# A block with causal attention: q's third parts and their stores go behind the first step's maxima, and a step's three rows of maxima go in one transfer

## The chip, the cores and the metric
The kernel runs on one core of one Trainium2 chip. The metric is the device time of one execution in microseconds; the time of a kernel is the median of its runs. Engines have queues of their own and run in the order written in the kernel; they meet through semaphores. TensorE multiplies matrices and transposes (PE in the profile, its weight loads PEld), VectorE is DVE, ScalarE is ACT, GpSimd is POOL, and SyncE (SP) issues nearly all DMA transfers.

## The reference
x is (2, 1024, 128): two batches of 1024 tokens, 16 heads of 8. In short:

```python
h = layernorm(x) * (1 + ca) + sa            # ca, sa, ga, cb, sb, gb: from silu(c) @ wmod
q, k, v = split(h @ qkv_w + qkv_b);  q, k = rotary(q), rotary(k)
attn = softmax(where(causal, q @ k.T / sqrt(8), -inf));  x = x + ga * ((attn @ v) @ out_w + out_b)
h = layernorm(x) * (1 + cb) + sb
x = x + gb * expert(h)                      # 8 experts of 64, one by argmax(h @ w_router); f = leaky(h @ w_fc) ** 2
```

## The kernel before
A **unit** is one batch b and one half of its 1024 query tokens; units are attended in the order (0,0), (0,1), (1,1), (1,0). A **step** is a unit and a group of 4 heads: 16 steps, of which 0 to 3 are unit (0,0), 4 to 7 unit (0,1). Scores are wanted close to float32, from bf16 matmuls. So q and k are each split into three bf16 parts that add up to the value, and the parts are stacked on partitions 0 to 71 of the tiles qst and kst, through a copy in HBM (qparts, kparts). Partitions 72 to 74 of qst hold the negated row maximum, again in three parts, against rows of ones in kst.

Each step has two passes. **Pass A** (`pass_a`, L1040 and L1045) makes the scores query by key, and VectorE reduces each PSUM bank of them to row maxima in tmax (L880). When the step's last bank is reduced, the stage `max1` makes negm (VectorE, L797) and splits it into three bf16 parts in negp, with four small operations of GpSimd (L535 to L538). The stage `max2` transposes negp (TensorE, L963), copies it to negt, 48 partitions by 128 (ScalarE, L631), and SyncE's `max_rows` sends negt to rows 72, 73 and 74 of qst (L450). **Pass B** (`pass_b`, L1062) makes the scores key by query with the maximum already taken off; ScalarE takes the exponential into pt (L676), GpSimd zeroes the future keys of diagonal blocks (L572), and `times_v` multiplies by v (L1082). TensorE's first matmul of pass B of a step waits for that step's rows of maxima.

`plan()` gives every bank of pass A (and of pass B) a **slot**, and every other stage a slot as well; each engine's queue is the slots in order, and within a slot the bank first, then the stages. Step 0 has the pass A slots 0 to 10, step 1 has 11 to 21, step 2 has 22 to 32. Pass B of step 0 takes slots 19 to 29, that of step 1 begins in slot 30. `max1` of step 0 is in slot 10, `max2` of step 0 in slot 16, `max1` of step 1 in slot 21, `max2` of step 1 in slot 25. TensorE does the matmuls of a stage one slot earlier, behind that slot's banks. Step 4 ends its pass A in slot 70; its pass B begins in slot 79, and v of unit (1,0) is in slot 82. Seven PSUM banks (`NB`) go round in the order in which TensorE uses them, whoever the user is: a bank can be written again when its user of seven places earlier has been read. Between slots without a bank of pass B TensorE does a filler matmul (L1024).

The stages q1, q2, q3 and k1, k2, k3 prepare a unit's q and k. q1: two matmuls (L952), two VectorE products into rot (L776), and their sum in full (GpSimd, L380). q2: cast to the first part (ScalarE, L619), remainder (GpSimd, L385). q3: cast to the second part (ScalarE, L623), remainder as the third part (GpSimd, L390), and the **stores** of q: `store` of SyncE waits for all three parts and issues eight transfers, two for each of the four groups of heads (L419 and L421). k is the same with four stores (L419). `load` brings a unit's stack from HBM to qst and kst, six transfers for a group (L441). For unit (0,1) the slots of these stages are written out by hand in `FIXED`; all others are looked for by `put`, which keeps GpSimd's longer stages apart. A stage of `FIXED` is placed where it says.

SyncE's queue is in the order of stages too: q3 of unit (0,1) (slot 8) with its eight stores, then the three rows of step 0 (slot 16), k3 (slot 22) with four stores, the three rows of step 1 (slot 25), the loads of group 0 (slot 25), and so on.

Of the kernel before, what the change touches and what calls it, by code (L numbers as in the profile page):

```python
# [29 lines left out]
P = 128  # L30
# [6 lines left out]
TU = HALF // P  # L37
HG = 4
NG = H // HG
PARTS = 3  # L40
ROWS = PARTS * PARTS * HD
ROWSM = ROWS + PARTS
# [30 lines left out]
def groups_b(half):  # L73

    out = []
    if half:
        out += [(kt, 0, 0, [(h, 1) for h in range(HG)]) for kt in range(TU)]
    for kt in range(TU):
        n = HALF - kt * P
        nh = max(1, HALF // n) if n < 384 else 1  # L80
        out.append((kt, half, kt * P, [(h, nh) for h in range(0, HG, nh)]))
    return out
# [17 lines left out]
POST_LAST = ["oT", "out", "st", "var2", "ln", "h2", "rt", "a0", "ohT", "a1", "m0", "a2", "m1", "a3", "m2", "y0", "m3", "y1"]  # L100
PREP_AT = [[0, 0], [40, 1], [93, 1]]
POST_AT = {("oT", (0, 0)): 81, ("a0", (0, 0)): 131}
FIXED = {("q1", (0, 1)): 3, ("q2", (0, 1)): 6, ("q3", (0, 1)): 8, ("k1", (0, 1)): 16, ("k2", (0, 1)): 19, ("k3", (0, 1)): 22}
MAX_LAG = 3
O_LAG = 3

# [12 lines left out]
def plan():  # L119
# [20 lines left out]
    def put(at, *stage):  # L140
# [3 lines left out]
        if need and stage[0] in HIDDEN + ("y0", "y1") and stage[1][0:2] == UNITS[-1]:  # L144
            hold = 1
        at = FIXED.get(stage, at)
        while stage not in FIXED and need and any(held.get(t, 0) + need > SIDES for t in range(at, at + hold)) \
                or stage not in FIXED and stage[0] != "max1" and any(t in pooled for t in range(at, at + busy)):
            at += 1
# [43 lines left out]
def adaln_block(nc, x, ct, wmod, wqkv, wsw, bcol, bv, wo, bo, wr, wfc, wpj, rope, out):  # L193
# [25 lines left out]
    with ExitStack() as ctx:  # L219
        def sb(name, shape, dt=F32):  # L220
            return ctx.enter_context(nc.sbuf_tensor(name, shape, dt))
# [4 lines left out]
        def sem(name):  # L226
            return ctx.enter_context(nc.semaphore(name))
# [45 lines left out]
        qst = sb("qst", [P, 2, H, HALF], BF16)  # L273
# [6 lines left out]
        negt = sb("negt", [PARTS * HG * TU, 2, P], BF16)  # L280
# [40 lines left out]
        s_mstack = [sem(f"s_mstack{i}") for i in range(2)]  # L321
# [19 lines left out]
        def side_ready(eng, st, k=0):  # L341
            ap, i, use = side(st, k)
            eng.wait_ge(s_side[i], use + 1)
            return ap, s_sfree[i]

        def wait_read(eng, name, u, k=0):

            _, i, use = side((name, u), k)
            eng.wait_ge(s_sfree[i], use + 1)

        def stored(eng, i, n, groups=0):

            eng.wait_ge(s_store[i], (2, 1)[i] * 16 * (NG * n + groups))
# [9 lines left out]
        def tiles(u):  # L363

            return PIECES[u[0:2]][u[2]]
# [27 lines left out]
        @block.sync  # L393
        def _(sp):
            sp.dma_start(xs[:, 0], x[0]).then_inc(s_ldx[0], 16)
            sp.dma_start(wqkv_sb[:, :], wqkv).then_inc(s_ldqkv, 16)
            sp.dma_start(wsw_sb[:, :], wsw).then_inc(s_ldqkv, 16)
            sp.dma_start(bcol_sb[:, :], bcol).then_inc(s_ldqkv, 16)
            for half in range(2):
                cols = slice(HALF * half, HALF * half + HALF)  # L400
                sp.dma_start(rope_sb[:, :, cols], rope[:, :, cols]).then_inc(s_ldrope[half], 16)
                if half == 0:
                    sp.dma_start(bv_sb[:, :], bv.partition_broadcast(P)).then_inc(s_ldbv, 16)
            for i in range(1, B * 2):
                sp.dma_start(xs[:, i], x[i]).then_inc(s_ldx[i], 16)
            sp.dma_start(bo_sb[:, :], bo.partition_broadcast(P)).then_inc(s_ldrest, 16)
            sp.dma_start(wo_sb[:, :], wo).then_inc(s_ldrest, 16)
            sp.dma_start(wr_sb[:, :], wr).then_inc(s_ldrest, 16)
            sp.dma_start(wfc_sb[:, :], wfc).then_inc(s_ldrest, 16)
            sp.dma_start(wpj_sb[:, :, :], wpj).then_inc(s_ldrest, 16)  # L410

            def store(u, i, groups):

                n, w = prep_no[u], 2 * u[0] + u[1]
                sp.wait_ge(s_part[i], 3 * (n + 1))
                for g in groups:
                    dst = (qparts, kparts)[i].ap()[w, g].rearrange("j d h t -> (d h) j t")
                    src = part[i][HG * HD * g:HG * HD * (g + 1)]
                    sp.dma_start(dst[:, 0:PARTS], src).then_inc(s_store[i], 16)  # L419
                    if i == 0:  # L420
                        sp.dma_start(dst[:, PARTS:5], src[:, 0:2]).then_inc(s_store[i], 16)  # L421

            def load(u, g):

                (b, half), w, n = u, 2 * u[0] + u[1], prep_no[u]
                if b:
                    sp.wait_ge(s_pv, group_no[(NG + g, len(groups_b(1)) - 1)] + 1)
                h0, row, R = HG * g, HG * HALF, PARTS * HD
                sp.wait_ge(s_ones, half + 1)
                sp.wait_ge(s_zeros, half + 1)  # L430
                if b:
                    sp.dma_start(qst[ROWS:ROWSM, half, h0:h0 + HG, :].rearrange("p h t -> p (h t)"),
                                 qst[ROWSM:ROWSM + PARTS, half, h0:h0 + HG, :].rearrange("p h t -> p (h t)")
                                 ).then_inc(s_stack[half][g], 16)
                for i, (dst, src, step) in enumerate(((qst, qparts, HD), (kst, kparts, 0))):
                    stored(sp, i, n, NG if n or g else 1)
                    planes = (5, PARTS)[i]
                    for p in range(PARTS):
                        rows = bass.AP(tensor=src, offset=((w * NG + g) * planes * HD + p * step) * row,
                                       ap=[[row, R], [1, HG * HALF]])  # L440
                        sp.dma_start(dst[R * p:R * p + R, half, h0:h0 + HG, :].rearrange("p h t -> p (h t)"),  # L441
                                     rows).then_inc(s_stack[half][g], 16)

            def max_rows(s):
                b, half, g = STEPS[s]
                wait_read(sp, "max2", s)
                M = HG * TU
                for p in range(PARTS):
                    dst = qst[ROWS + p:ROWS + p + 1, half, HG * g:HG * g + HG, :].rearrange("o h (r x) -> o (h r) x", x=P)
                    sp.dma_start(dst, negt[M * p:M * p + M, s % 2, :]).then_inc(s_mstack[s % 2], 16)  # L450

            def run(st):
                if st[0] in ("q3", "k3"):
                    first = st[1] == (0, 0)
                    store(st[1], 0 if st[0] == "q3" else 1, range(1 if first else NG))
                if st[0] == "load":
                    load(st[1], st[2])
                    if st[1:] == ((0, 0), 0):
                        for i in range(2):
                            store((0, 0), i, range(1, NG))  # L460
                if st[0] == "max2":
                    max_rows(st[1])
                if st[0] == "y1":
                    u, (t0, t1) = st[1], tiles(st[1])
                    wait_read(sp, "y1", u)
                    sp.dma_start(out[2 * u[0] + u[1], :, t0:t1], y[:, t0:t1]).then_inc(s_out, 16)

            for st in order:
                run(st)
            sp.wait_ge(s_out, 16 * sum(len(p) for p in PIECES.values()))  # L470
# [114 lines left out]
        def _(act):  # L585
# [22 lines left out]
            def run(st):  # L608
# [17 lines left out]
                if name == "max2":  # L626
                    s = u
                    src, free = side_ready(act, st)
                    if s >= 2:
                        act.wait_ge(s_mstack[s % 2], 48 * (s // 2))  # L630
                    act.activation(negt[:, s % 2, :], src[0:PARTS * HG * TU, 0:P // 2].bitcast(BF16),  # L631
                                   ACT.Copy).then_inc(free, 1)
                if name == "o":
                    s = u
# [43 lines left out]
            for st in PRE:  # L678
                run(st)
# [206 lines left out]
        def _(pe):  # L886
# [163 lines left out]
            def pass_b(i):  # L1050

                s, gi, (kt, kh, c0, _), (h0, nh), _ = b_at[i]
                b, half, g = STEPS[s]
                n, w = bank_no[i], HALF - c0
                if n == 0:
                    pe.wait_ge(s_ones, 1)
                if gi == 0 and h0 == 0:
                    pe.wait_ge(s_mstack[s % 2], 48 * (s // 2 + 1))
                dst = take("b", i)
                for j in range(nh):  # L1060
                    h = HG * g + h0 + j
                    last = pe.matmul(dst[:, j * w:(j + 1) * w], kst[:, kh, h, kt * P:kt * P + P],  # L1062
                                     qst[:, half, h, c0:HALF], start=True, stop=True)
                last.then_inc(s_b, 1)
# [89 lines left out]
```

## Time and profile before

| | us |
|---|---|
| median of 3 runs (lowest, highest) | 366.17 (365.56, 366.2) |
| the profiled execution | 365.83 |
| its span, first to last instruction | 364.1 |
| PE busy | 333.2 (92% of the span) |
| DVE busy | 257.9 (71%) |
| ACT busy | 207.7 (57%) |
| POOL busy | 110.9 (30%) |

The profiled execution is 1.7 us longer than its span. Busy time of PE is the time in which any matmul is open; matmuls overlap, so that their starts lie closer than their durations (a 512-column one has 0.38 us, and the next starts 0.22 us after it).

### The profile page before, as it was taken

The numbers are of one execution on the slowest core, as the hardware profiler recorded it, in microseconds if no ns is written. First come the engines' busy times: TensorE is split into PE (matmuls) and PEld (weight loads), VectorE is DVE, ScalarE is ACT, GpSimd is POOL, SyncE is SP. The second block draws the span as 40 slices with busy tenths as digits, with TensorE's granted clock in tenths as the row PEclk, the third lists the DMA queues.
The fourth block names the chain that finished last, engine by engine and source line by source line (L and its number), as shares of the span: only waits on it lengthen the run. The fifth ranks groups of instructions, "written<-read, shape, count | busy, mean of one in ns | idle before, by whom it ended". The sixth has DMA issues, their size and how long they took to land.

```text
span 364.1 us, 6867 instructions
## 1 busy us (share of the span) xinstructions
PE 333.2 (92%) x2320; PEld 163.3 (45%) x2360; DVE 257.9 (71%) x563; ACT 207.7 (57%) x399; POOL 110.9 (30%) x191
## 2 busy tenths in 40 slices
PE   6999779998889899999999989999999999899886
PEld 3645335443443333453543535444435445435555
DVE  3764787888899987777777888677888777423254
ACT  5160146755157565778456765864777666686241
POOL 3927453437401413601301212101204132344121
PEclk9999989999999999999999999999999999999999
DMA  6527704220510003140220400400000000000000
GB/s 208 181 62 198 169 23 111 69 66 2 139 46 0 3 1 74 42 137 0 69 81 17 119 16 2 136 0 31 1 2 3 3 3 1 4 0 3 29 2 29
DMA packets 13362, 18.97 MB, mean 52 GB/s; under 512 B 4216, under 2 KB 9208, under 8 KB 13328
## 3 DMA queue, kind: packets, MB, share of 16 engines
q1 hardware_dynamic: 13040, 18.14, 18.6%
q8 instruction: 19, 0.31, 0.4%
q10 hardware_dynamic: 288, 0.39, 0.3%
q14 instruction: 15, 0.12, 0.1%
HBM read 12.98 MB, written 5.24 MB: 50 GB/s over the span
## 4 chain that ended last, share of the span: by engine, by line
PE 60%; issue 9%; DVE 9%; POOL 3%; ACT 3%; another core or an unknown queue 2%; SPq 1%; DMA 1%; ACTq 0%; POOLq 0%; DVEq 0%
PE ps_o L1082 16%; PE ps L1045 13%; PE ps L1062 12%; PE ps L1016 4%; DVE tmax L880 4%; PE ps L1003 4%; PE ps L1040 2%; PE ps L952 1%; ACT pt L676 1%; PE ps L1009 1%; PE ps L1024 1%; DVE rot L776 1%; PE ps L943 1%; DMA qst<-negt 1%
## 5 line engine op out<-in xcount | busy, mean ns | idle before, releaser
L880 DVE TENSOR_REDUCE tmax<-ps 128x1 f32<-128x512 f32 (+3 forms) x304 | 185.7, 655 | 60.1 <-PE ps L1045 57.7
L676 ACT ACTIVATE pt<-ps 128x512 f32<-128x512 f32 (+1 forms) x304 | 161.3, 576 | 100.0 <-PE ps L1062 86.3
L1045 PE MATMUL ps<-kst,qst 128*128 128x128 bf16 (+3 forms) x566 | 110.1, 273 | 4.3 <-DVE tmax L880 2.4
L1062 PE MATMUL ps<-qst,kst 128*128 128x512 bf16 (+3 forms) x368 | 105.2, 326 | 5.8 <-DVE rot L776 1.8
L1082 PE MATMUL ps_o<-pt,v_sb 128*32 128x512 f32 (+3 forms) x768 | 78.7, 496 | 2.7 <-ACT pt L676 1.4
L1045 PEld LDWEIGHTS ps<-kst,qst 128*128 128x128 bf16 x576 | 49.6, 99 | 65.7 <-DVE tmax L880 16.1
L572 POOL TENSOR_SCALAR_AFFINE_SELECT pt<-pt 128x512 f32<-128x512 f32 x64 | 40.2, 638 | 65.1 <-ACT pt L676 64.7
L1062 PEld LDWEIGHTS ps<-qst,kst 128*128 128x128 bf16 x384 | 35.0, 98 | 32.1 <-issue 8.0
L1024 PE MATMUL ps<-maska,identb 128*128 128x512 bf16 x120 | 35.4, 402 | 3.5 <-POOL maska L491 3.3
L535 POOL CAST negp<-negm 128x16 bf16<-128x16 f32 x16 | 3.1, 196 | 92.5 <-DVE negm L797 92.3
L1082 PEld LDWEIGHTS ps_o<-pt,v_sb 128*32 128x32 f32 x768 | 16.9, 108 | 29.2 <-ACT pt L676 16.3
L1040 PE MATMUL ps<-maska,identb 128*128 128x512 bf16 x54 | 21.2, 392 | 0.4 <-DMA kst<-kparts 0.4
L516 POOL TENSOR_TENSOR rstd<-veps,mhalf 128x4 f32<-128x4 f32 (+1 forms) x9 | 8.5, 949 | 37.1 <-DVE veps L738 36.9
L1024 PEld LDWEIGHTS ps<-maska,identb 128*128 128x128 bf16 x124 | 12.6, 103 | 15.6 <-POOL maska L491 3.3
L1003 PE MATMUL ps<-h2t,wfc_sb 128*128 128x512 f32 (+1 forms) x40 | 16.9, 520 | 0.0
L856 DVE TENSOR_TENSOR fg<-ps,fg 128x512 f32<-128x512 f32 (+1 forms) x20 | 11.4, 578 | 7.6 <-PE ps L1009 4.6
L619 ACT ACTIVATE part<-full 128x512 bf16<-128x512 f32 x8 | 5.0, 628 | 20.6 <-POOL full L380 15.4
L1016 PE MATMUL ps<-wpg,fg 128*128 128x128 f32 x128 | 16.1, 279 | 0.6 <-DVE fg L856 0.6
L1016 PEld LDWEIGHTS ps<-wpg,fg 128*128 128x128 f32 x128 | 15.1, 192 | 3.1 <-ACT pt L676 1.7
L380 POOL TENSOR_TENSOR full<-rot 128x512 f32<-128x512 f32 x6 | 7.6, 1266 | 25.2 <-DVE rot L776 25.2
L655 ACT ACTIVATE fg<-ps 128x512 f32<-128x512 f32 (+1 forms) x20 | 10.3, 513 | 2.2 <-PE ps L1003 1.9
L776 DVE SCALAR_TENSOR_TENSOR rot<-ps,bcol_sb,rope_sb 128x512 f32<-128x512 f32 x16 | 11.3, 742 | 0.0
(103 smaller groups left out, 259.3 us busy)
## 6 DMA issues: line engine op xcount, KB each, us to landing
qst<-qparts SPq DMA_DIRECT2D x48, 96.0 KB
kst<-kparts SPq DMA_DIRECT2D x48, 96.0 KB
qparts<-part SPq DMA_DIRECT2D x16, 96.0 KB, 1.9
kparts<-part SPq DMA_DIRECT2D x16, 96.0 KB, 1.9
xs<-in_x SPq DMA_DIRECT2D x4, 256.0 KB, 7.2
rope_sb<-in_rope SPq DMA_DIRECT2D x2, 512.0 KB, 6.3
qparts<-part SPq DMA_DIRECT2D x16, 64.0 KB, 1.8
qst<-negt SPq DMA_DIRECT2D x48, 4.0 KB, 1.7
```

Source lines behind the costliest of these rows:

```text
L572: pool.affine_select(out=d, in_=d, compare_op=ALU.is_ge, fill=0.0, base=0, pattern=[[0, HG], [1, P]], channel_multiplier=-1).then_inc(s_tr ...
L676: act.activation(pt[:, G % NP, h0:h0 + nh, 0:w], src, ACT.Exp, scale=SCALE).then_inc(s_exp, 1)
L776: dve.scalar_tensor_tensor(out=rot[i][:, j], in0=src, scalar=bcol_sb[:, 2 * i + j:2 * i + j + 1], in1=rope_sb[:, j, HALF * u[1]:HALF * u[1 ...
L856: dve.tensor_tensor(fg[:, c, cols], src[:, cols], fg[:, c, cols], ALU.mult).then_inc(free, 1)
L880: dve.tensor_reduce(dst, src, AX.X, ALU.max).then_inc(s_max, 1)
L1003: pe.matmul(dst[:, cols], wfc_sb[:, P * c:P * c + P], h2t[:, cols], start=True, stop=True).then_inc(full_, 1)
L1016: last = pe.matmul(dst[:, D * t:D * t + D], fg[:, c, P * t:P * t + P], wpg[:, u[0], c], start=(c < c1), stop=(c == c1))
L1024: pe.matmul(ps[:, reached[0] % NB, :], identb[:, :], maska[:, :, :].rearrange("p h k -> p (h k)"), start=True, stop=True)
L1040: pe.matmul(dst, identb[:, :], maska[:, :, :].rearrange("p h k -> p (h k)"), start=True, stop=False, skip_group_check=True)
L1045: last = pe.matmul(dst[:, j * nk:(j + 1) * nk], qst[:, half, h, r * P:r * P + P], kst[:, kh, h, k0:k0 + nk], start=(kind != "diag"), stop= ...
L1062: last = pe.matmul(dst[:, j * w:(j + 1) * w], kst[:, kh, h, kt * P:kt * P + P], qst[:, half, h, c0:HALF], start=True, stop=True)
L1082: last = pe.matmul(ps_o[32 * j:32 * j + 32, 0, c0:HALF], v_sb[:, TU * (2 * b + kh) + kt, c:c + 32], pt[:, G % NP, j, 0:HALF - c0], start=( ...
```

## The change
There are two edits. In `FIXED`, q3 of unit (0,1) goes from slot 8 to slot 18. This moves ScalarE's cast to the second part, GpSimd's remainder and SyncE's eight stores behind `max1` and `max2` of step 0; on GpSimd the remainder is now between k1's sum and k2's remainder, on SyncE the stores are just ahead of k3's. Nothing else changes its slot. In `max_rows`, the loop over three transfers of one row (16 partitions of negt each) becomes one transfer of three rows (48 partitions), for all 16 steps; the semaphore rises by 16 instead of 48 and its two waiters follow.

```diff
-FIXED = {("q1", (0, 1)): 3, ("q2", (0, 1)): 6, ("q3", (0, 1)): 8, ("k1", (0, 1)): 16, ("k2", (0, 1)): 19, ("k3", (0, 1)): 22}
+FIXED = {("q1", (0, 1)): 3, ("q2", (0, 1)): 6, ("q3", (0, 1)): 18, ("k1", (0, 1)): 16, ("k2", (0, 1)): 19, ("k3", (0, 1)): 22}
...
             def max_rows(s):
                 b, half, g = STEPS[s]
                 wait_read(sp, "max2", s)
-                M = HG * TU
-                for p in range(PARTS):
-                    dst = qst[ROWS + p:ROWS + p + 1, half, HG * g:HG * g + HG, :].rearrange("o h (r x) -> o (h r) x", x=P)
-                    sp.dma_start(dst, negt[M * p:M * p + M, s % 2, :]).then_inc(s_mstack[s % 2], 16)
+                dst = qst[ROWS:ROWSM, half, HG * g:HG * g + HG, :].rearrange("p h (r x) -> p (h r) x", x=P)
+                sp.dma_start(dst, negt[:, s % 2, :]).then_inc(s_mstack[s % 2], 16)
...
-                        act.wait_ge(s_mstack[s % 2], 48 * (s // 2))
+                        act.wait_ge(s_mstack[s % 2], 16 * (s // 2))
...
-                    pe.wait_ge(s_mstack[s % 2], 48 * (s // 2 + 1))
+                    pe.wait_ge(s_mstack[s % 2], 16 * (s // 2 + 1))
```

## Rows read from the trace of the kernel before

**Rows 1.** The page, busy time, share of the span, instructions
```profile
PE 333.2 (92%) x2320; PEld 163.3 (45%) x2360; DVE 257.9 (71%) x563; ACT 207.7 (57%) x399; POOL 110.9 (30%) x191
```
**Rows 2.** Waits of PE, whole span: us in total, times, longest
```profile
PE ps L1062 <- DMA qst<-negt: 1.3, 1, 1.3
```
**Rows 3.** Timeline, PE, 40 to 60 us: start, us, [idle before <-releaser]
```profile
43.05 0.24 PE L963 MATMUL ps<-identb,negp 128*48 128x128 bf16 x1 [2.42 <-POOL negp L538]
...
46.51 0.33 PE L1045 MATMUL ps<-kst,qst 128*128 128x384 bf16 x1
49.08 0.37 PE L1045 MATMUL ps<-kst,qst 128*128 128x384 bf16 x1 [2.25 <-DVE tmax L880]
...
53.24 0.24 PE L963 MATMUL ps<-identb,negp 128*48 128x128 bf16 x1
...
58.75 0.34 PE L1045 MATMUL ps<-kst,qst 128*128 128x384 bf16 x1
59.22 0.39 PE L1062 MATMUL ps<-qst,kst 128*128 128x512 bf16 x1
```
**Rows 4.** Windows of 0.5 us: us, PE busy, PEclk, DMA share, GB/s
```profile
47.50:48.00 0.50, 0.00 (x0) 1.00 0.06 8
...
49.00:49.50 0.50, 0.42 (x2) 0.72 0.00 0
...
52.50:53.00 0.50, 0.50 (x9) 0.86 0.00 0
```
**Rows 5.** Timeline, DVE, 40 to 50 us
```profile
40.27 0.19 DVE L797 TENSOR_REDUCE negm<-tmax 128x16 f32<-128x32 f32 x1
...
45.46 0.69 DVE L880 TENSOR_REDUCE tmax<-ps 128x2 f32<-128x512 f32 x1 [2.01 <-PE ps L1045]
46.07 1.40 DVE L776 SCALAR_TENSOR_TENSOR rot<-ps,bcol_sb,rope_sb 128x512 f32<-128x512 f32 x2
47.38 1.61 DVE L880 TENSOR_REDUCE tmax<-ps 128x4 f32<-128x512 f32 x3
```
**Rows 6.** Timeline, POOL, 40 to 52 us
```profile
40.85 1.15 POOL L390 TENSOR_TENSOR part<-rot,part 128x512 bf16<-128x512 f32 x1 [0.80 <-ACT part L623]
41.95 0.20 POOL L535 CAST negp<-negm 128x16 bf16<-128x16 f32 x1
...
42.78 0.22 POOL L538 TENSOR_TENSOR negp<-negr,negp 128x16 bf16<-128x16 f32 x1
47.60 1.26 POOL L380 TENSOR_TENSOR full<-rot 128x512 f32<-128x512 f32 x1 [4.60 <-DVE rot L776]
50.54 1.16 POOL L385 TENSOR_TENSOR rot<-full,part 128x512 f32<-128x512 f32 x1 [1.68 <-ACT part L619]
```
**Rows 7.** Timeline, ACT, 43 to 51 us
```profile
43.33 0.27 ACT L631 ACTIVATE negt<-ps 48x128 bf16<-48x128 bf16 x1 [2.62 <-PE ps L963]
49.28 0.60 ACT L676 ACTIVATE pt<-ps 128x512 f32<-128x512 f32 x1 [5.68 <-remote]
49.77 0.62 ACT L619 ACTIVATE part<-full 128x512 bf16<-128x512 f32 x1
50.29 1.07 ACT L676 ACTIVATE pt<-ps 128x512 f32<-128x512 f32 x2
```
**Rows 8.** Timeline, SP, DMA issues, 42 to 56 us (eight L419 and L421, first shown)
```profile
42.03 0.32 SPq L419 DMA_DIRECT2D qparts<-part  x1
...
45.78 1.88 SPq L450 DMA_DIRECT2D qst<-negt  x3
54.44 1.75 SPq L419 DMA_DIRECT2D kparts<-part  x4
```
**Rows 9.** The chain that ended last, at 57 us: start, us, what
```profile
57.43 1.74 DMA qst<-negt
```
**Rows 10.** Timeline, PE, 101 to 103 us
```profile
101.14 0.39 PE L1062 MATMUL ps<-qst,kst 128*128 128x512 bf16 x1 [1.32 <-DMA qst<-negt]
...
102.68 1.16 PE L956 MATMUL ps<-wqkv_sb,ht 128*128 128x128 f32 x8
```
**Rows 11.** Timeline, DVE, from 98 us
```profile
98.36 5.46 DVE L880 TENSOR_REDUCE tmax<-ps 128x1 f32<-128x512 f32 x9
```

## The prediction
> **What bounds the kernel now.** I read the page first, for how much TensorE time there is: matmuls are open for 92% of the span [rows 1]. A place where TensorE stands still is therefore paid for in full unless another engine is as late there. Then I read the waits of TensorE for the change's own transfer: the trace names one, of 1.3 us [rows 2]. A list of releasers can hide what stands at the head of a queue, so I read TensorE in order of time around the first step [rows 3]. The reader is to see two pauses. The transposition of step 0's maxima (L963) comes 2.42 us late, released by GpSimd. Then nothing starts between the last matmul of pass A at 46.51 and 49.08; the trace names VectorE, but VectorE had handed on that bank long before. What lies ahead of it in TensorE's queue is slot 19's first matmul of pass B, which waits for the rows of maxima. The third of those transfers starts about 1.2 us after 45.78 and lands 1.74 us after that [rows 8, 9], at some 48.8; the 49.08 agrees. The granted clock falls right behind this pause, in the half microsecond from 49.0 (0.72), and is back only after 52.5 [rows 4].
>
> So step 0's maxima are one chain: VectorE's last reduction, four small GpSimd operations, transpose, copy by ScalarE, rows to qst. Three links of it are late. On GpSimd the q remainder (L390, 40.85 to 42.00) stands ahead of them though the maxima are there at 40.46 [rows 5, 6]. On SyncE eight stores of q stand ahead of the rows: the copy is ready at 43.60 [rows 7], the first row is issued at 45.78 [rows 8]. And there are three issues, 1.88 us, instead of one.
>
> **The move, up to the rows of step 0.** With q3 in slot 18, GpSimd is free at 40.46. Its handover from VectorE is 0.13 us elsewhere (46.07 + 1.40 = 47.47 to 47.60) [rows 5, 6], so the split of the maxima starts at 40.59 instead of 41.95: 1.36 us earlier. TensorE's transpose comes at 41.69, ScalarE's copy ends at 42.24, and SyncE has nothing else to issue: the row transfer starts at 42.27. With k1's matmuls shifted alike, TensorE comes to slot 19's pass B at 46.51 + 0.16 - 1.36 = 45.3.
>
> **The transfer.** 1.74 us is the landing of a 4 KB row [rows 9]. What one of 12 KB with 48 packets takes the trace does not show. Below: the same 1.74, if it spreads over 16 engines as each row does. Above: while three rows move, the 16 engines are busy 0.06 of the time at 8 GB/s [rows 4]; that is 0.48 engine-us for 16 packets of 256 B, 0.03 us each. With 16 packets in a row on one engine 0.45 us come on top (2.2 us), with all 48 on one 1.4 us (3.2 us). Today the third row lands 2.9 us after the first issue. I take 1.74 to 2.2: landed at 44.0 to 44.5, ahead of 45.3 in either case. The Trainium skill, DMA: Bandwidth & Descriptors, section on why a DMA increments its semaphore by 16, states that the number of engines is the largest up to 16 that divides the slowest dimension of both sides; here those are 3 and 48, so three engines where each old row had 16. It speaks against merging; by it the landing is the 2.2 us, and the sum below loses 0.04 us.
>
> **What is late next.** The pause was also time in which others caught up, so I follow all queues to step 1's transpose. VectorE reduces bank 16 at 45.46 - 1.36 = 44.10, does k1's two products until 46.11, then banks 17 to 19 (1.61 us) and 20, 21 (0.5 us each), and has step 1's maxima at 48.8 [rows 5]. GpSimd: k1's sum (L380, 1.26 us) from 46.24 to 47.50; now the moved q remainder (L390, 1.15) to 48.6; k's first remainder (L385, 1.16) to 49.75; then step 1's four small operations (41.95 to 43.00, 1.05 us) to 50.8 [rows 6]. ScalarE: exponentials of slot 19 near 45.8; then its cast of k (L619, 0.62) must wait for GpSimd's 47.50, which it did not before, and the exponentials of slots 20 and on stand behind it until 48.15, which is still 2.1 us earlier than before [rows 7]. Its moved cast of q (L623, 0.6 us like L619) stands in the gap behind the copy, before slot 19, and costs nothing; that gap is from 42.24 to 45.7. TensorE runs out of banks on the way several times by 0.1 to 0.5 us and then waits for step 1's split: its second transpose comes at 50.85 instead of 53.24 [rows 3]. The shift is **2.39 us**, set by GpSimd's queue, no longer by TensorE. If the q remainder were not in this queue it would be more by up to 1.15.
>
> SyncE: q's eight stores take 3.75 us (42.03 to 45.78) [rows 8]. Now they run from 48.65 to 52.40, with nothing behind them but k's stores. Those waited for GpSimd's k3 before; GpSimd ends L385 at 49.75 instead of 51.70, so they start at 54.44 - 1.95 = 52.5 and end at 54.3. The one row transfer of step 1 starts there and lands at 56.1 to 56.5. Before, it landed at 57.43 + 1.74 = 59.17 and TensorE, through with its pass A of 58.75 (0.16 us in the stream), could have gone on at 58.91 but did at 59.22 [rows 3, 9]. With the shift it asks at 56.52. So this wait of **0.31 us** goes too, or all but 0.04 of it. The loads of unit (0,1) stand behind this on SyncE; they come earlier too.
>
> **Later steps.** At 101.14 stands the one wait that the trace puts on the rows, 1.32 us [rows 2, 10]. One transfer lands 0.7 to 1.2 us earlier. I count this at **zero**: VectorE has nine reductions without a gap from 98.36 to 103.82, the banks that TensorE takes next come free only through them, and v's matmuls at 102.68 take the bank of slot 79, whose reduction is the seventh of these (about 102.0 to 102.6) [rows 10, 11]. If that cover is not as tight as I read it, up to 0.5 us more is won. The other thirteen row transfers show no wait; a shorter one is worth nothing there. After step 1 the order of work is the old one on all queues and nothing is tied to absolute time, so the shift should last to the end.
>
> **Sum.** 2.39 + 0.31 + 0 = 2.7 us. The profiled execution is 365.83 us with a span of 364.1; I expect a span of 361.4. Against the median of the runs, 366.17, that gives 363.5.
>
> **The rivals.** (a) *The clock.* The one pause before 43.05 left the clock at full, the second one brought it down [rows 3, 4]. Afterwards there are pauses of 1.1 us (before 41.7) and, from 45.5 to 50.85, several small ones with a last one of about 1.7 us; only half of that stretch is matmul work. If the clock falls there and stays low as long as it did (49.2 to 52.6, 3.4 us), up to 3.4 us of matmuls run at half speed where TensorE is the bound again: 1.7 us back, 365.2. Against it: a pause of 2.4 us alone did not do it. The Trainium skill, TensorE: Matmul & The Clock Gate, Part 1, says the same way round that activity releases a throttle which is the default. (b) *A queue longer than I make it.* From 46 to 51 GpSimd is busy nearly all the time, and ScalarE waits for it; if handovers or a bank cost 1 us more, the gain is 1.4 to 1.9 us: 364.5. (c) *Hidden anyway.* If the merged transfer or a later stretch bound by VectorE takes the gain, the time is 366.0. For it speaks only that step 4 does so locally; against it, that VectorE itself starts earlier. (d) *Slower: the merged transfer is slow.* It decides at 2.9 us from issue to landing, what three rows take now. At 3.2 us (all packets on one engine) no step loses more than 0.3 us. At 4.5 us each of the 16 steps would be up to 1.6 us later; if four of them have no slack, 6.4 are paid against 2.7 won: 369.9; two such steps give 366.7. No row has a transfer this small at such a time.
>
> **Chances.** Forecast (363.5, own range 362.6 to 364.3) 0.62; (a) 0.15; (b) 0.12; (c) 0.06; (d) 0.05. Some 0.2%, 0.7 us, is what a measurement can tell here; (a) and (b) are below 365.44 and count as faster: 0.89 faster, 0.06 same, 0.05 slower. The range goes down by the 0.5 us of step 4 and a shorter GpSimd queue, up to (a): 362.6 to 365.2.
>
> **What would show it.** Step 0's negp cast right behind the negm reduction, about 40.6; one row issue at 42.3; the first exponential at about 45.8 instead of 49.28; clock at 1.00 through 49 to 53; L390 of q between L380 and L385 at 47.5; second transpose near 50.9, no wait at the pass B of step 1. Landing of qst from negt between 1.7 and 2.2. VectorE still without a gap from 96 to 101. The forecast is wrong if the clock falls behind 46, if landing is above 2.9, or if the distance between the traces at 60 us is not there any more at the end.

## The result, and the profile after

| | before | after |
|---|---|---|
| median of five runs (lowest, highest) | 366.17 (365.29, 366.92) | 363.12 (361.05, 363.51) |
| the profiled execution | 365.83 | 361.05 |
| its span | 364.1 | 359.3 |
| PE busy | 333.2 | 334.0 |

The ratio is 0.9924, with an interval of 0.9895 to 0.9952: 1.8 to 3.8 us faster. 363.5 was forecast. But the two profiled executions differ by 4.8 us of span, not by 2.7, so the first question is where the rest lies. The timeline of PE at the start of the kernel, before (first fence) and after (second); columns as in [rows 3]:

```profile
6.30 1.71 PE L924 MATMUL ps<-silu,wmod_sb 128*128 128x2 f32 x8
7.86 1.87 PE L1024 MATMUL ps<-maska,identb 128*128 128x512 bf16 x4
```
```profile
6.29 0.95 PE L922 MATMUL ps<-silu,wmod_sb 128*128 128x2 f32 x8
7.10 1.02 PE L1022 MATMUL ps<-maska,identb 128*128 128x512 bf16 x4
```

Line numbers of after are lower by two. The same eight matmuls start at the same time and take 1.71 us in one execution and 0.95 in the other. This is long before anything that the change touches, and it carries on: VectorE reduces step 0's maxima at 40.27 before and at 37.56 after, 2.71 us apart. The kernels below, most of which have the move or the merged transfer too, speak against an effect of the change (last section). So from here on all times are counted from this reduction of step 0, called **zero** below; what the change does is read from the distances behind it.

The timelines of DVE, SP, ACT, POOL and PE after, the lines that answer to [rows 5], [rows 8], [rows 7], [rows 6] and [rows 3]:

```profile
37.56 0.19 DVE L795 TENSOR_REDUCE negm<-tmax 128x16 f32<-128x32 f32 x1
...
45.82 0.19 DVE L795 TENSOR_REDUCE negm<-tmax 128x16 f32<-128x32 f32 x1
```
```profile
39.49 0.88 SPq L448 DMA_DIRECT2D qst<-negt  x1
45.87 0.34 SPq L419 DMA_DIRECT2D qparts<-part  x1
...
49.80 1.89 SPq L419 DMA_DIRECT2D kparts<-part  x4
51.74 0.77 SPq L448 DMA_DIRECT2D qst<-negt  x1
```
```profile
42.95 0.60 ACT L674 ACTIVATE pt<-ps 128x512 f32<-128x512 f32 x1 [2.97 <-PE ps L1060]
44.76 0.63 ACT L617 ACTIVATE part<-full 128x512 bf16<-128x512 f32 x1 [1.21 <-POOL full L380]
45.29 1.55 ACT L674 ACTIVATE pt<-ps 128x512 f32<-128x512 f32 x3
```
```profile
43.47 1.26 POOL L380 TENSOR_TENSOR full<-rot 128x512 f32<-128x512 f32 x1 [4.60 <-DVE rot L774]
44.68 1.16 POOL L390 TENSOR_TENSOR part<-rot,part 128x512 bf16<-128x512 f32 x1
45.80 1.16 POOL L385 TENSOR_TENSOR rot<-full,part 128x512 f32<-128x512 f32 x1
46.90 0.20 POOL L533 CAST negp<-negm 128x16 bf16<-128x16 f32 x1
```
```profile
38.92 0.24 PE L961 MATMUL ps<-identb,negp 128*48 128x128 bf16 x1 [1.00 <-POOL negp L536]
...
48.00 0.24 PE L961 MATMUL ps<-identb,negp 128*48 128x128 bf16 x1 [1.51 <-POOL negp L536]
...
53.52 0.34 PE L1043 MATMUL ps<-kst,qst 128*128 128x384 bf16 x1
54.02 0.39 PE L1060 MATMUL ps<-qst,kst 128*128 128x512 bf16 x1 [0.17 <-DMA qst<-negt]
```

The first transposition stands 1.36 us behind zero; before it was 2.78. The rows leave at 1.93. From 46.90 on step 1's own four operations follow GpSimd's three long ones without a gap, and the second transposition stands at 10.44, where it was 12.97: 2.53 us. The windows of 1 us around it (columns: stretch, us, busy time of PE, PEld, DVE, ACT and POOL, then PEclk, DMA share and GB/s as in [rows 4]) have the clock at full throughout, also behind the pause of TensorE:

```profile
46.00:47.00 1.00, 0.49 (x5) 0.21 (x5) 1.00 (x3) 0.86 (x3) 1.00 (x2) 1.00 0.25 59
47.00:48.00 1.00, 0.00 (x0) 0.00 (x0) 0.80 (x2) 1.00 (x3) 0.78 (x5) 1.00 0.54 134
48.00:49.00 1.00, 1.00 (x11) 0.60 (x15) 0.18 (x1) 0.39 (x2) 1.00 (x2) 1.00 0.69 171
```

The chain that ended last has the merged transfer of step 1, and PE at step 4 the wait that answers to [rows 10]; the third fence is DVE there [rows 11]:

```profile
51.26 0.44 SPq L419
51.69 0.04 issue
51.74 2.24 DMA qst<-negt
53.98 0.05 issue
54.02 0.39 PE ps L1060
```
```profile
95.26 0.39 PE L1060 MATMUL ps<-qst,kst 128*128 128x512 bf16 x1 [0.64 <-DMA qst<-negt]
...
97.49 1.16 PE L954 MATMUL ps<-wqkv_sb,ht 128*128 128x128 f32 x8 [0.20 <-DVE tmax L878]
```
```profile
92.57 6.06 DVE L878 TENSOR_REDUCE tmax<-ps 128x1 f32<-128x512 f32 x10
```

At step 1's first matmul of pass B the traces are 2.49 us apart (18.95 and 16.46 behind zero), at step 4's reduction of maxima 2.48, at step 15's 2.45. Nothing is given back in between. From the last reduction to the end this execution loses 0.36 us (323.83 against 321.74 from zero to the end, 2.09 apart; the second profile of the same kernel below has 2.28). 2.71 of the start and 2.09 behind zero are the 4.8 us.

The 0.36 us are lost behind the kernel's last instruction that the view shows, SyncE's last store of the result. The timelines of SP at the end, before and after:

```profile
361.12 1.22 SPq L466 DMA_DIRECT2D out<-y  x2
```
```profile
355.95 1.23 SPq L464 DMA_DIRECT2D out<-y  x2
```

From the end of this row to the end of the span there are 1.76 us before (362.34 to 364.1) and 2.12 after (357.18 to 359.3). All seven profiles of kernels with the merged transfer, the six below and this one, have 2.08 to 2.17 us there; all four with three transfers have 1.73 to 1.78. So the merged transfer costs some 0.35 us at the end of the program. Why it does is not shown.

### The profile page after: what moved, and what is told of

Read it like the earlier page. It is cut to its first block, busy times and chain, and to the rows that moved or that the text cites. A ratio compares the mean times of both kernels' runs of the same rounds, so it can differ in the third digit from the quotient of the medians.

```text
span 359.3 us, 6875 instructions
## 1 busy us (share of the span) xinstructions
PE 334.0 (93%) x2360; PEld 160.3 (45%) x2360; DVE 258.5 (72%) x563; ACT 207.7 (58%) x399; POOL 111.0 (31%) x191
## 4 chain that ended last, share of the span: by engine, by line
PE 64%; DVE 10%; issue 10%; POOL 2%; ACT 2%; SPq 1%; DMA 1%; ACTq 0%; DVEq 0%; POOLq 0%
PE ps_o L1080 17%; PE ps L1060 13%; PE ps L1043 13%; PE ps L1014 4%; DVE tmax L878 4%; PE ps L1001 4%; PE ps L1038 3%; PE ps L950 2%; PE ps L1022 1%; PE ps L1007 1%; DVE rot L774 1%; PE ps L941 1%; SPq L419 1%; ACT pt L674 1%; PE ps L968 1%
## 5 line engine op out<-in xcount | busy, mean ns | idle before, releaser
L1060 PE MATMUL ps<-qst,kst 128*128 128x512 bf16 (+3 forms) x384 | 110.3, 326 | 4.7 <-DVE rot L774 2.2
L1043 PE MATMUL ps<-kst,qst 128*128 128x128 bf16 (+3 forms) x576 | 113.2, 274 | 0.7 <-DVE fg L854 0.3
L570 POOL TENSOR_SCALAR_AFFINE_SELECT pt<-pt 128x512 f32<-128x512 f32 x64 | 40.3, 639 | 64.5 <-ACT pt L674 64.2
L1022 PE MATMUL ps<-maska,identb 128*128 128x512 bf16 x124 | 35.4, 393 | 3.3 <-POOL maska L489 3.3
L1038 PE MATMUL ps<-maska,identb 128*128 128x512 bf16 x64 | 24.5, 382 | 0.2 <-DVE tmax L878 0.2
```

What stands on the lines that cost most here:

```text
L570: pool.affine_select(out=d, in_=d, compare_op=ALU.is_ge, fill=0.0, base=0, pattern=[[0, HG], [1, P]], channel_multiplier=-1).then_inc(s_tr ...
L1022: pe.matmul(ps[:, reached[0] % NB, :], identb[:, :], maska[:, :, :].rearrange("p h k -> p (h k)"), start=True, stop=True)
L1038: pe.matmul(dst, identb[:, :], maska[:, :, :].rearrange("p h k -> p (h k)"), start=True, stop=False, skip_group_check=True)
L1043: last = pe.matmul(dst[:, j * nk:(j + 1) * nk], qst[:, half, h, r * P:r * P + P], kst[:, kh, h, k0:k0 + nk], start=(kind != "diag"), stop= ...
```

## The experiments

In the table each kernel's profiled execution, counted from zero: the two transpositions of step 0's and step 1's maxima (T0, T1), step 1's first matmul of pass B (B1), and how much earlier than in the kernel before step 4's and step 15's reductions of maxima come. Then the time, against runs of the kernel before of the same series. Those had a median of 365.89 beside change_again, move_only, merge_only and q_slot16, 365.96 beside k_late, k_late_rows3 and warm_wait, and 364.69 beside q_slot16_b and k_later, so medians of different series are not to be compared directly.

| kernel | zero at | T0 | T1 | B1 | step 4 | step 15 | median | ratio |
|---|---|---|---|---|---|---|---|---|
| before | 40.27 | 2.78 | 12.97 | 18.95 | 0 | 0 | 366.17 | |
| the change | 37.56 | 1.36 | 10.44 | 16.46 | 2.48 | 2.45 | 363.12 | 0.9924 (0.9895 to 0.9952) |
| change_again | 38.05 | 1.36 | 10.46 | 16.30 | 2.63 | 2.64 | 361.72 | 0.9904 (0.9869 to 0.9939) |
| move_only | 40.17 | 1.36 | 10.46 | 17.11 | 1.82 | 1.82 | 362.27 | 0.9915 (0.9883 to 0.9948) |
| merge_only | 39.76 | 2.78 | 11.80 | 17.60 | 1.33 | 1.34 | 365.18 | 0.9981 (0.9958 to 1.0003) |
| q_slot16 | 39.84 | 1.36 | 10.18 | 15.94 | 3.00 | 2.97 | 361.9 | 0.9893 (0.9858 to 0.9928) |
| q_slot16_b | 39.87 | 1.36 | 10.19 | 15.97 | 2.96 | 2.89 | 362.67 | 0.9925 (0.99 to 0.995) |
| k_late | 39.86 | 1.36 | 9.63 | 15.93 | 2.74 | 2.71 | 361.47 | 0.9895 (0.9864 to 0.9927) |
| k_late_rows3 | 37.82 | 1.37 | 9.63 | 15.94 | 2.71 | 2.66 | 362.88 | 0.9905 (0.9872 to 0.9938) |
| k_later | 39.88 | 1.37 | 9.64 | 14.43 | 3.61 | 3.56 | 362.21 | 0.9921 (0.9893 to 0.9949) |
| warm_wait | 39.68 | 2.79 | 12.43 | 18.89 | -0.06 | -0.84 | 366.65 | 1.0031 (1.0 to 1.0062) |

The medians are blunter than the distances, because the start of the kernel scatters by some 2 us (last section). Where they can't tell two kernels apart, the distances decide below, and that is said. In k_late, k_late_rows3 and k_later the first matmul of pass B of step 1 has no record; its start is taken as 0.22 us ahead of the matmul of pass A behind it (k_late 56.01, k_late_rows3 53.98, k_later 54.53). In k_late and k_late_rows3 v's matmuls stand ahead of B1 and in k_later behind it, so that B1 is not to be compared with the others'.

**The whole change again**, unchanged, to see what repeats.

> The changed kernel again, beside the three others on one chip. Both theories: 10.4 us from step 0's negm to the second transpose and 16.5 to pass B of step 1, whatever the start of the kernel does. The time of the profiled execution had 2.7 us of its 4.8 us from before step 0's maxima, where the change does nothing; the theory is that this is TensorE's clock coming up at another moment (11 us before, 6.3 us after by the matmul durations), and that the five times fall in two groups 2 us apart as they did (361.05, 361.57 and 363.12, 363.32, 363.51). Rival: the change itself makes the start faster; then the profile shows negm of step 0 at 37.6 again in every run of it, and those of the kernel before at 40.3.

Measured: 1.36, 10.46, 16.30 at B1 and 2.63 at step 4. The list of waits has none of TensorE for step 1's rows here, but there still is one of 0.17 us. PE:

```profile
54.02 0.34 PE L1043 MATMUL ps<-kst,qst 128*128 128x384 bf16 x1
54.35 0.39 PE L1060 MATMUL ps<-qst,kst 128*128 128x512 bf16 x1
```

TensorE could have gone on at 54.02 + 0.16 = 54.18. The rows were issued at 52.06; with the 2.24 us of the first profile they land at 54.30, and 0.05 us later the matmul starts, as at 54.02 in that profile. The rows left 14.01 us behind zero here and 14.18 there, where one store of q took 0.60 us of SyncE instead of 0.43 and the four of k 1.89 instead of 1.81. So the distances of one kernel repeat within 0.2 us (2.45 and 2.64 at step 15). The zero of 38.05 is early again, as the rival has it; the last section comes back to that. The times are 361.36 to 361.85 in four executions and 363.41 and 363.45 in two.

**The move alone:**

```diff
-... ("q3", (0, 1)): 8, ...
+... ("q3", (0, 1)): 18, ...
```

> The move alone: q3 of unit (0,1) in slot 18, three transfers of one row per step as before. I count from step 0's negm reduction, so that what lies before it drops out: to the second transpose it was 12.97 us before and 10.44 with both edits; to the first matmul of pass B of step 1 18.95 and 16.46. Theory (the GpSimd queue sets the second transpose, the three rows of step 0 are in time anyway: last one landed at 45.2 in the clock of the old profile, wanted at 45.3): 10.4 to 10.6 to the transpose, the same as with both. Pass B of step 1 then waits for the third row behind k's stores, about 0.7 us later than with both: 17.2. Time 0.6 to 0.8 us above the change, about 364.0 beside 366.2. Rival (merging and moving are worth about the same, each its part): the transpose comes only about 1.2 us sooner than before, 11.7, time near 364.9.

Measured: 1.82 us at step 4 and constant, clock 1.00; T1 is where the whole change has it, as the theory says. The chain that ended last at step 1:

```profile
54.30 0.51 SPq L450
...
54.85 0.59 SPq L450
...
55.50 1.74 DMA qst<-negt
57.24 0.05 issue
57.28 0.39 PE ps L1062
```

TensorE waits 0.81 us for the third row. Its zero is at 40.17, like that of the kernel before: the moved stage alone does not bring the early start.

**The merged transfer alone:**

```diff
-... ("q3", (0, 1)): 18, ...        # of the kernel after
+... ("q3", (0, 1)): 8, ...
```

> The merge alone: q3 stays in slot 8, its eight stores ahead of step 0's rows. Theory: the row transfer is issued as late as before and lands 2.24 us after issue (measured with the change) against 2.9 for the third of three, so pass B of step 0 starts 0.7 us sooner; to the second transpose 12.2 to 12.4 us instead of 12.97, to pass B of step 1 about 18.0 instead of 18.95; nothing at step 4. Time 0.7 to 1.0 us below the kernel before, about 365.3. Rival (the shorter pause keeps TensorE's clock at full, and that is the larger part): to pass B of step 1 under 17.3, time 1.6 us or more below. Rival (the merged transfer is on three engines and slower than it saves): no gain, 366.2.

Measured: T1 1.17 us sooner than before, where the theory had 0.6 to 0.8, and 1.33 at step 4. The pause of TensorE still lasts from 46.00 to 47.68, but the clock does not fall behind it, as the windows of 2 us show:

```profile
46.00:48.00 2.00, 0.64 (x4) 0.22 (x3) 2.00 (x5) 0.00 (x0) 0.91 (x1) 1.00 0.05 12
48.00:50.00 2.00, 2.00 (x19) 1.22 (x17) 1.97 (x6) 1.91 (x4) 1.00 (x2) 1.00 0.04 8
...
349.00:353.00 4.00, 4.00 (x14) 2.50 (x13) 0.98 (x7) 2.30 (x7) 0.32 (x1) 0.57 0.00 0
```

To split the 1.17: slot 19's first matmul of pass B has no record in the trace of before. The matmul behind it starts at 49.08 [rows 3], and in merge_only those two starts are 0.22 us apart (47.68 and 47.90), so it stood at some 48.86, 8.59 behind zero. Here it stands at 7.92: 0.67 us from the transfer. The other 0.50 come by T1, in the stretch that ran at the lower clock before: 0.63 us for a 512-column matmul there, 0.38 here. The last line shows that this execution met the lower clock elsewhere, in its tail. From step 15's reduction to the end it loses 1.55 us against before, 1.17 of them at the lower clock and the rest behind the last store, so that its end is 0.21 us later than that of before (324.04 against 323.83 from zero). The median's ratio, 0.9981, leaves open whether merging alone is faster at all; by the distances it is, up to the tail.

**q's third parts in slot 16** instead of 18, everything else as after, run twice:

```diff
-... ("q3", (0, 1)): 18, ...
+... ("q3", (0, 1)): 16, ...
```

> The change with q3 of unit (0,1) in slot 16 instead of 18: still behind step 0's maxima and rows on every queue, but ahead of k1's sum on GpSimd, where the queue stood empty for 4.6 us. Theory (the GpSimd queue between k1's sum and step 1's maxima sets the second transpose): L390 of q leaves that queue, 1.15 us; the transpose comes at 9.3 to 9.4 us from step 0's negm (10.44 with the change), where VectorE's negm of step 1 (8.26) is the bound; to pass B of step 1 15.2 to 15.4 (16.46). Time 1.1 us below the change, about 362.0. Rival (TensorE's banks through ScalarE's exponentials behind its cast of k set it): no difference from the change beyond 0.2 us.

> q3 in slot 16 again, beside the other on one chip, because its gain over the change (0.3 to 0.5 us by negm of step 4) is below what the times of one series tell. Theory (GpSimd's queue, 0.3 us of it q's remainder): second transpose at 10.18 again and step 4's negm 2.97 us ahead of the kernel before. Rival (the 0.3 us was a chance of one profile): 10.4 and 2.5 to 2.6.

Measured: T1 at 10.18 and 10.19, 3.00 and 2.96 us at step 4. The timeline of POOL:

```profile
42.41 1.16 POOL L390 TENSOR_TENSOR part<-rot,part 128x512 bf16<-128x512 f32 x1 [1.26 <-ACT part L621]
45.75 1.26 POOL L380 TENSOR_TENSOR full<-rot 128x512 f32<-128x512 f32 x1 [2.18 <-DVE rot L774]
47.81 1.16 POOL L385 TENSOR_TENSOR rot<-full,part 128x512 f32<-128x512 f32 x1 [0.80 <-ACT part L617]
48.91 0.20 POOL L533 CAST negp<-negm 128x16 bf16<-128x16 f32 x1
```

The remainder now lies in GpSimd's idle time ahead of k1's sum. That takes 1.16 us out of the queue behind it, yet T1 gains only 0.26: between k's sum and k's remainder GpSimd waits 0.80 us for ScalarE's cast of that sum. In the changed kernel q's remainder filled just that wait. The theory (T1 at 9.3 to 9.4) had it cost its whole duration in slot 18; that falls. B1 is 0.33 to 0.52 us sooner than after's two profiles, because the stores are out of the way too. The medians of the two runs of this kernel, 361.9 and 362.67, lie between the two of the change, 361.72 and 363.12, so they can't tell the kernels apart.

**k behind step 1's maxima too** (merged transfer; k_late_rows3 is the same slots with the three transfers of before):

```diff
-... ("q3", (0, 1)): 18, ("k1", (0, 1)): 16, ("k2", (0, 1)): 19, ("k3", (0, 1)): 22}
+... ("q3", (0, 1)): 16, ("k1", (0, 1)): 16, ("k2", (0, 1)): 22, ("k3", (0, 1)): 25}
```

> Built on the change: q3 of unit (0,1) in slot 16, k2 from 19 to 22 and k3 from 22 to 25, so that GpSimd has nothing of k between k1's sum and the split of step 1's maxima, and step 1's row transfer is ahead of k's four stores on SyncE. With q3 in slot 16 alone the second transpose came 10.18 us after step 0's negm, not at the 9.35 that I expected: GpSimd waited 0.80 us for ScalarE's cast of k, which the q remainder had filled before. Theory: k2's remainder and that wait are what is left, VectorE's negm of step 1 (8.26) becomes the bound; second transpose at 9.3 to 9.4, pass B of step 1 at 15.1 to 15.3, time 0.7 us below q3 in slot 16 alone. Rival: k's late preparation holds something else up (v of unit (0,1) moves from slot 27 to 30, the loads of unit (0,1) from 25 to 26), and the gain is gone by the first load or by step 4: no difference in time from q3 in slot 16.

> The same slots as the run before it, with three transfers of one row per step as in the kernel before. It asks what merging is worth once no stores stand ahead of the rows of steps 0 and 1. Theory: nothing; the third row lands some 2.9 us after the first issue instead of 2.24, and at step 0 and step 1 both are in time (pass B of step 0 at 5.0 us, of step 1 at 15.1 to 15.3 from step 0's negm), so the two differ by less than 0.3 us in time. Rival: the 0.66 us later landing holds up pass B of step 1 or a later step: 0.4 to 0.7 us slower than with one transfer.

Measured: T1 at 9.63 in both, 1.36 us behind step 1's reduction of maxima (8.27), just as T0 is behind step 0's. So VectorE, not GpSimd's long operations, sets it now; the 9.3 to 9.4 expected left too little for the split. But only 2.74 and 2.71 us are left at step 4, less than with q3 in slot 16 alone: the rival came true. PE of k_late has a new wait:

```profile
53.01 0.39 PE L1060 MATMUL ps<-qst,kst 128*128 128x128 bf16 x4
53.85 0.85 PE L1080 MATMUL ps_o<-pt,v_sb 128*32 128x384 f32 x8 [0.46 <-POOL pt L570]
```

k's last remainder (GpSimd, 51.97 to 53.13) now stands ahead of a diagonal block's mask, and the multiplication by v waits for that mask. And once step 1's rows have no stores ahead of them, merging gains nothing that can be measured at step 4 (0.03 us). From zero to the end k_late is even the longer one, 321.54 us against 321.18, by the 0.35 us or so behind the last store.

**k's last remainder two slots later still**, behind that mask:

```diff
-... ("k3", (0, 1)): 25}             # of k_late
+... ("k3", (0, 1)): 27}
```

> The k_late kernel with k3 of unit (0,1) in slot 27 instead of 25 (v of that unit goes to slot 32 with it). With k3 in slot 25 the second transpose came 9.63 us after step 0's negm, bound by VectorE's negm of step 1 as expected, but from step 3's negm on it stood at 2.71 us ahead of the kernel before, less than the 2.97 with q3 in slot 16 alone; its profile has a wait of 0.46 us of TensorE's multiplication by v for GpSimd's mask, which stood behind k3's remainder. Theory: k3 two slots later lets that mask through first; second transpose unchanged at 9.6, step 4's negm 3.2 to 3.5 us ahead of the kernel before. Rival: the wait only moves to another mask or to v, and step 4's negm stays at 2.7 to 2.8.

Measured: T1 the same, the wait for the mask is gone, 3.61 us at step 4 (3.2 to 3.5 expected) and 3.56 at step 15, 320.62 from zero to the end. By the distances this is the best of the kernels, about 1 us ahead of the change. The times don't settle it: its median of 362.21 is 0.46 us below that of q_slot16_b in its series, less than either kernel scatters. In its PE timeline the multiplication by v has no wait any more:

```profile
53.36 0.85 PE L1080 MATMUL ps_o<-pt,v_sb 128*32 128x384 f32 x8
54.14 0.71 PE L1043 MATMUL ps<-kst,qst 128*128 128x384 bf16 x2
```

**The old pause kept warm.** Before, with nine filler matmuls (no part of the result) put into the pause, to measure what the clock alone was worth:

```diff
+                if i == min(b_at):
+                    keep_warm(9)
                 if i in b_at:
                     pass_b(i)
```

> The kernel before with nine filler matmuls of 512 columns on TensorE between pass A of slot 19 and the first matmul of pass B, about 1.9 us inside the 2.2 us in which it waits for the rows. No wait is shortened. It measures what the fall of the clock behind that pause is worth. Theory (the clock is a small part of the gain; the second transpose was held by GpSimd behind the late exponentials): clock at full from 49 to 53 us; pass B of step 0 unchanged at 8.97 us from negm; second transpose at 12.3 to 12.7 instead of 12.97; time 0.3 to 0.7 us below the kernel before. Rival (much of what the change won is the clock kept at full): second transpose under 12.0, time 1 us or more below.

Measured: clock 1.00 from 46 to 54 us, slot 19's first matmul of pass B at 8.54 (the expectation's 8.97 is the second one; here it stands at 8.92), T1 at 12.43 instead of 12.97. With 8.59 for before that is 0.49 us for the clock, the same as merge_only gave. It is not all that TensorE wins: its last matmul ahead of T1 starts at 10.99 instead of 12.71, and then it waits 1.11 us for GpSimd's split, which comes at the old time. At B1 0.06 us is left. The timelines of PE there and at step 4, and SP at step 4:

```profile
58.57 0.39 PE L1062 MATMUL ps<-qst,kst 128*128 128x512 bf16 x1 [0.61 <-DMA qst<-negt]
...
101.37 0.39 PE L1062 MATMUL ps<-qst,kst 128*128 128x512 bf16 x1 [2.08 <-DMA qst<-negt]
```
```profile
97.67 2.53 SPq L450 DMA_DIRECT2D qst<-negt  x3
```

The stores of k and three row issues do not come sooner with TensorE, so the gain is lost in the wait for step 1's rows. At step 4 the three issues happened to take 2.53 us here, where they take 1.77 in the trace of before; the wait grew by the same 0.76, from 1.32 [rows 10] to 2.08, and from step 5 on the kernel is 0.66 us later than up to step 4. The cover that holds step 4's wait of 1.3 us at no cost does not hold 2.1. The time was expected 0.3 to 0.7 us below the kernel before and was not: 366.65 against 365.96, ratio 1.0031. The profile explains the end of its own execution only. In nine of the twelve executions the mean clock was below 1 (0.991 or 0.995), so in most of them it fell somewhere all the same; no trace shows where, and why the median is higher stays open.

## Why the prediction was right, and which terms were not

**How close the number is.** The time was forecast at 363.5 and measured at 363.12. A part of that is luck. The five executions of the change were two of 361.05 and 361.57 and three of 363.12 to 363.51; the median is one of the upper three, and the same kernel gave 361.72 the next time. The distances are the better test: of 2.70 us forecast, 2.45 and 2.64 are there at step 15 and 2.09 and 2.28 at the end.

**The bound and the pause.** Right: the pause behind pass A was the transfer of step 0's rows behind q's stores. merge_only shortens it by the transfer alone and move_only by the queue alone, and both move T1.

**The move.** Rows were forecast to leave 2.00 us behind zero and left at 1.93; GpSimd's order and the handover of ScalarE's exponentials came as worked out (the exponentials go on at 7.73 behind zero, forecast 7.9). The shift of the second transposition was 2.39 us by forecast and 2.53 in the trace, set by GpSimd's queue as said: TensorE stands idle for 1.51 us ahead of it and is released by L536, the last of GpSimd's four operations. Some 0.5 us of this shift is the clock that no longer falls, by warm_wait and merge_only; the kernel before had that loss in its T1. The side remark that the queue would gain "up to 1.15 more" without q's remainder is wrong in size: 0.26, since 0.80 us of waiting for ScalarE's cast takes its place (q_slot16). I had counted k's first remainder as ready to start when the remainder of q ended, and that hid the wait. Nor do the prediction's own times allow 1.15: with step 1's maxima at 48.8, a handover of 0.13 and a split of 1.05 the transposition comes at 50.0 at the earliest, 0.8 us sooner than 50.85.

**The transfer: the number is right, the reason is not.** The merged one landed after 2.24 us, near the upper value of 1.74 to 2.2, where one row takes 1.74 [rows 9] and still does in move_only. The upper value was 0.45 us for 16 packets in a row on one engine. Windows of 0.1 us (stretch, us, PEclk, DMA share, GB/s) show how long the data moves, first for step 0's merged transfer after, then for the third row of step 4 before:

```profile
41.00:41.10 0.10, 1.00 0.23 51
41.10:41.20 0.10, 1.00 0.24 54
```
```profile
100.60:100.70 0.10, 1.00 0.16 26
100.70:100.80 0.10, 1.00 0.12 16
```

By the trace's records of single packets, the 48 packets of the merged transfer run in three streams, 0.014 us from one packet of a stream to the next, with three packets of 4 bytes at their ends; a row's 16 packets have 16 of 4 bytes. That fits three engines where a row has 16. By the Trainium skill, DMA: Bandwidth & Descriptors, section on why a DMA increments its semaphore by 16, the dimensions 3 and 48 give three engines; the trace agrees with it. But the split costs little. At step 1 the merged transfer has its first packet 1.40 us after issue, moves data for 0.27 and lands 0.57 after that; a row has 1.23, 0.16 and 0.35. So of the 0.50 us only 0.11 is data on fewer engines; 0.17 lies ahead of the first packet and 0.22 behind the last. That 0.45 was so near is luck. What the other 0.39 us come from is open, as no transfer of the same bytes over 16 engines was run. Its issue takes 0.70 to 0.77 us (0.88 at step 0), against 0.51 to 0.59 for each of three rows that take 1.77 together.

**Step 1's wait: the term that was mis-sized.** The prediction has "this wait of 0.31 us goes too, or all but 0.04 of it". It measures -0.04 us in the first profile (2.53 at T1, 2.49 at B1) and +0.14 in the second. TensorE came to it as forecast: pass A at 53.52 + 0.16 = 53.68, 5.68 us behind T1, forecast 5.67. But the rows left 14.18 behind zero where 14.0 was forecast, landed 2.24 later instead of 1.74 to 2.2, and T1 was 0.14 us earlier than forecast, so that TensorE asked at 16.12 for what landed at 16.42. In the second profile the rows left at 14.01, as forecast, and the wait is 0.17 us. The forecast had it at nothing or 0.04. Two chains meet here. One runs through GpSimd and TensorE's queue, the other through k's stores on SyncE, and both moved by about 2.5 us; the later one still is SyncE's, as it was before. So the gain up to step 4 is 2.48 to 2.63, where 2.70 was forecast; 0.07 to 0.22 too much.

**The end: a term that was missing.** The prediction says that the shift should last to the end. It lasts to the last store; behind it each kernel with the merged transfer is some 0.35 us longer than those with three. So 2.09 and 2.28 us remain of 2.70.

**Step 4 at zero.** Right: TensorE's wait fell from 1.32 to 0.64 us and the distance did not change; VectorE goes through ten reductions without a gap (92.57 to 98.63, for the nine of [rows 11]), and v waits for its bank. The prediction looked only for what could be won there. warm_wait suggests, from one profile, that something could be lost: three issues that take 0.76 us longer cost 0.66. One transfer gives that place some margin.

**The rivals.** (a) The clock did not fall behind the new pauses, 1.00 in all profiles of the change. What it had cost before at T1 is measured twice, 0.50 and 0.49 us. It was no term of its own in my sum, and needed none, since GpSimd's queue sets T1 once it is gone. (b) and (c) fall by the distance of 2.5 to 2.6 us that is constant up to step 15. (d) falls by the 2.24 us; it would have decided at 2.9. That the change speeds up the start of the kernel, which both its profiles would suggest, is weakened by k_late_rows3, which has the early start too, and by the change's own executions, of which five of eleven took the longer times; it is not ruled out by a profile of the change with a late start.

**Are the two parts worth their sum?** No: 1.82 and 1.33 alone, 2.5 to 2.6 together. Both shorten the same wait at step 0. Added to the move, the transfer is worth 0.66 to 0.81 up to step 4 (step 1's third row), of which 0.29 and 0.48 are left at the end (322.03 us from zero with the move alone, 321.74 and 321.55 with both). With step 1's stores out of the way as well it wins 0.03 and loses 0.36 at the end. Three transfers with k_later's slots were not run; by these numbers they may be the better choice.

## What to carry to other kernels

Count times from the last event that the change can't touch, not from the start of the span: here over half of the 4.8 us between two profiles was there before it. When a pause goes away, follow every queue to the next meeting point and take the later chain, and before an operation that is moved is charged with its full duration, look for the wait on another engine that it would fill. Small transfers are worth merging where their issues stand on the path; elsewhere it won nothing here, and it cost 0.35 us at the end of the program. So compare two traces up to the very end, too.

## What the runs showed of the hardware beyond that

**The start of the kernel goes one way or the other.** Step 0's reduction of maxima stands at 39.7 to 40.3 in eight profiled executions (before, move_only, merge_only, both of q_slot16, k_late, k_later, warm_wait) and at 37.6 to 38.1 in three (both of the change, k_late_rows3). In the first eight the eight matmuls at some 6.30 us take 1.70 or 1.71 us, in the change's two 0.95, in k_late_rows3 1.22. 1.71 to 0.95 is about the ratio of TensorE's two levels (2.4 and 1.2 GHz), so the clock rises at another moment of the same instructions. The profile's clock column reads 1.00 there in every case: it shows nothing ahead of the first recorded change, and durations have to be read. The times of many kernels fall in two groups some 2 us apart as well, the six of q_slot16 being 360.69, 360.92, 360.98 and 362.83, 362.98, 363.32; those of k_later, q_slot16_b and warm_wait do not fall apart so clearly. What decides it is open. k_late, with the late start, and k_late_rows3, with the early one, differ in the number of row transfers; the change has the early one in both its profiles, and merging alone has the late one. So neither edit alone goes with it. Only the change's own pair of edits has never been seen with the late start, in two profiles; that its times fall in both groups is the reason to take this for chance.

**The lower clock can turn up elsewhere**: merge_only's granted clock was 0.57 from 349 to 353 us, behind idle times of 0.46 and 0.27 us among float32 matmuls (346.5 to 347.4). The change has idle times of 0.45 and 0.27 at the same place and a clock of 1.00 there. One trace shows it, at a cost of 1.17 us. It is hardly rare: ten of merge_only's twelve executions have a mean clock of 0.994 or 0.995, though only this trace says where.

**One issue of SyncE is not always the same**: three row issues take 1.77 to 1.79 us at steps 1, 3 and 4 of the four kernels that have them, 1.98 to 2.19 at step 2, 2.16 to 2.37 at step 5 and 1.86 to 1.88 at step 0. In warm_wait they took 2.53 at step 4 and 2.45 at step 7, where the others have 1.82.
